# Running the shift matmuls of a block before the weight contraction of an older block on TensorE

## The reference

```python
value = (xf @ vp_w.T + vp_b).reshape(n, L, G, cg)
om_in = conv_general_dilated(x, dw_w, (1, 1), 'SAME', feature_group_count=c, ...) + dw_b
om = om_in... @ om_w.T + om_b            # per pixel, 8 groups, 9 taps: offsets y and x, mask
py = row + base_y + off_y;  px = column + base_x + off_x
y0 = floor(py);  x0 = floor(px);  ty = py - y0;  tx = px - x0
sampled = bilinear(value at y0, y0+1, x0, x0+1)   # zero outside the image
out = einsum('nhwgk,nhwgkc->nhwgc', mask, sampled)
out = out.reshape(n, L, c) @ op_w.T
```

## Time and profile before

| | |
|---|---|
| median of 3 runs | 2999.73 us (2999.16 to 3000.77) |
| profiled execution | 2998.01 us, span 2996.1 us |
| TensorE busy | 2713.6 us, 91% of the span |
| VectorE busy | 2195.8 us, 73% |
| ScalarE busy | 2107.3 us, 70% |
| GpSimd busy | 1924.4 us, 64% |
| first `windows` to last | 785 to 2962 us of the span |

### The profile page before, as it was taken

How to read it: one execution, slowest core, us unless ns; L and a number is a source line. 1 busy time by engine, 2 the same in 40 slices (tenths; PEclk the granted TensorE clock), 3 DMA queues, 4 the chain that set the end, 5 groups by cost and what they waited for, 6 DMA issues and landing times. The chain is left out here.

```text
span 2996.1 us, 99369 instructions
## 1 busy us (share of the span) xinstructions
PE 2713.6 (91%) x40456; PEld 2166.3 (72%) x40456; DVE 2195.8 (73%) x3108; ACT 2107.3 (70%) x4273; POOL 1924.4 (64%) x1451
## 2 busy tenths in 40 slices
PE   5888859996599999999999999999999999999998
PEld 3555536774388787877878787777778787778786
DVE  4454533334688897989898888989897988889763
ACT  2334326662778787887878787887878787878782
POOL 2000000001788888888988888888888888888892
PEclk9999979998799999999999999999999999999999
DMA  4344459995477777777778786777777787777675
GB/s 109 97 117 108 129 124 264 266 266 158 133 192 205 189 210 194 202 198 193 203 194 215 192 209 184 214 191 200 204 191 199 192 215 189 208 189 210 172 183 153
DMA packets 343609, 558.99 MB, mean 187 GB/s; under 512 B 159184, under 2 KB 245712, under 8 KB 342992
## 3 DMA queue, kind: packets, MB, share of 16 engines
q1 hardware_dynamic: 284112, 461.96, 61.2%
q10 hardware_dynamic: 59136, 91.76, 8.6%
HBM read 351.36 MB, written 202.19 MB: 185 GB/s over the span
## 5 line engine op out<-in xcount | busy, mean ns | idle before, releaser
L1277 PE MATMUL acc_p<-abuf,vbd 128*32 128x170 f32 (+9 forms) x20480 | 1033.4, 370 | 10.7 <-issue 9.6
L1277 PEld LDWEIGHTS acc_p<-abuf,vbd 128*32 128x32 f32 (+1 forms) x20480 | 819.4, 144 | 216.4 <-issue 30.0
L1110 ACT ACTIVATE dwt<-xp,wts 128x224 f32<-128x224 f32 x2016 | 803.1, 488 | 41.0 <-ACT wst L1134 32.3
L981 DVE TENSOR_TENSOR pr<-mh_p,ht 128x864 f32<-128x864 f32 x672 | 669.2, 1052 | 23.2
L243 PE MATMUL cv<-cin,wb 128*64 128x392 bf16 x6912 | 603.1, 338 | 26.0 <-ACT cin L222 26.0
L1254 PE MATMUL win_p<-pr,smat 128*128 128x160 f32 x4032 | 612.0, 306 | 12.6 <-POOL pr L1067 10.9
L1254 PEld LDWEIGHTS win_p<-pr,smat 128*128 128x128 f32 x4032 | 557.6, 191 | 38.5 <-issue 13.3
L243 PEld LDWEIGHTS cv<-cin,wb 128*64 128x64 bf16 x6912 | 409.7, 112 | 213.4 <-ACT cin L222 26.2
L1050 POOL TENSOR_TENSOR dwt<-dwt 128x896 f32<-128x896 f32 x224 | 518.8, 2316 | 4.7 <-ACT dwt L1110 4.7
L1064 POOL TENSOR_TENSOR pr<-pr 128x576 f32<-128x576 f32 x224 | 317.0, 1415 | 211.5 <-DVE pr L981 211.5
L971 DVE TENSOR_TENSOR mh_p<-oms,ht 128x864 f32<-128x864 f32 x224 | 395.3, 1765 | 7.1 <-ACT ht L1125 7.1
(11 more groups left out here) (132 smaller groups left out, 2581.2 us busy)
## 6 DMA issues: line engine op xcount, KB each, us to landing
abuf<-weight_scratch SPq DMA_DIRECT2D x784, 240.0 KB, 4.1
weight_scratch<-wst ACTq DMA_DIRECT2D x112, 800.0 KB, 5.1
xt<-x SPq DMA_DIRECT2D x128, 392.0 KB, 7.6
rows_scratch<-vsb SPq DMA_DIRECT2D x224, 128.0 KB, 3.1
vbd<-rows_scratch SPq DMA_DIRECT2D x896, 32.0 KB, 4.5
x_scratch<-xt SPq DMA_DIRECT2D x64, 392.0 KB, 6.7
y<-x SPq DMA_DIRECT2D x64, 392.0 KB, 5.3
x3h<-x_scratch SPq DMA_DIRECT2D x64, 392.0 KB, 5.7
```

Of the source, the lines that this page charges most:

```text
L981: dve.tensor_tensor(pr[:, j % 2, slots, :, :, :].rearrange("p k e x z -> p e k (x z)"), mh[:, a, :, :].rearrange("p (k x) z -> p k (x z)", ...
L1110: ins = act.activation(dwt[:, j % 2, k, :].rearrange("p (r w) -> p r w", w=W), image[:, r:r + BR, k % 3:k % 3 + W], ACT.Identity, scale=dw ...
L1277: mm = pe.matmul(acc_p[32 * (2 * s + b):32 * (2 * s + b) + 32, 0:2 * TN].rearrange("p (k w) -> p k w", w=W)[:, k0:k1 + 1, x0:x1], vbd[0:K, ...
```

## The change

In `step` of TensorE in `l1_pass` the call of `windows` moves ahead of that of `apply`:

```diff
                 def step(i, j, first, last):
+                    windows(i, j)
                     n = near(i, j, -5 if j % 2 else -4, first, last)
                     if n:
                         apply(*n, j % 2)
-                    windows(i, j)
                     offsets_and_misc(phase(i, j), i + 1 if j == GROUPS_AT and not last else None,
                                      near(i, j, 2, first, last), near(i, j, -LAG, first, last), near(i, j, 3, first, last))
```

## The result

| | median, us | runs, us | span of the profiled execution, us |
|---|---|---|---|
| before | 2999.44 | 4, 2996.04 to 3000.77 | 2996.1 |
| changed | 3039.76 | 4, 3035.53 to 3043.59 | 3035.8 |

The ratio is 1.0136 with a 95% interval of 1.0118 to 1.0153: some 41 us slower.

The account below looks back on a forecast made before the run. TensorE was taken as the bound, idling mostly before offsets_and_misc behind GpSimd's depthwise sum. Merge 27, load 21 and clock -2 sum to +46 us: 3044 for the profiled execution, 3046 as median, range 3013 to 3072.

Parts of the forecast that it names:

- clock, spells after: TensorE, step 9 after the change: spells at 1.2 GHz in 7 to 15 pairs, 0.95 us each; 10 us.
- clock, spells before: TensorE, step 9 before the change: seven spells at 1.2 GHz, 1.7 us lost each, credited to the change as -12 us.
- First step, the merge: Steps 9 and 10: windows, now first, waits for GpSimd's late merge; 1.79 us in each of 15 pairs, 27 us.
- Step 8 adds none: Step 8: no loss from the merge, since offsets_and_misc waits there for VectorE's L962, which comes at its old time.
- That step 4 costs nothing: Step 4 ends 1.32 us later, but mask_hats in step 5 still ends behind GpSimd's L1050; 0 us added.
- Second step, the load: SyncE, step 6: the next images' last quarter is issued some 3.5 us later, so VectorE waits in step 7; 21 us.
- if the transfers land as much faster: Lower bound of the load term: transfers issued later land correspondingly faster, so the load costs 0 instead of 21 us.
- Third step, the clock: TensorE around step 9: spells at 1.2 GHz before and after the change nearly cancel; -2 us, between -12 and +2.
- Rival 1: Step 7: the load lands in time anyway, leaving +25 us, 3025; chance 0.22.
- Rival 2: ScalarE's weight copies in odd steps become the wait, their cover being only 0.55 us; 3080 to 3100 us, chance 0.08.
- Rival 3: TensorE's waits only move from offsets_and_misc to windows, nothing to be seen: within 6 us of 3000; chance 0.07.
- Rival 4: VectorE's mask_hats falls between GpSimd's operations, 97 us less VectorE work in the backlog, so faster: 2949; chance 0.08.

Follow-up runs that it names:

- e6b: Changed kernel with step 6's image load issued ahead of its weight read and ten filling matmuls ahead of windows in step 9: 3011.61 us, ratio 1.0046.
- e1: Changed kernel with SyncE issuing step 6's load of the next images ahead of its weight read: 3022.17 us, ratio 1.0092.
- e2: Changed kernel with ten filling matmuls on TensorE ahead of windows in step 9: 3020.69 us, ratio 1.0088.
- e10: Kernel before with eight filling matmuls of 160 columns ahead of offsets_and_misc in step 9: 2998.60 us, ratio 1.0010.
- e4: Kernel before with the new order (windows ahead of apply) in step 9 of each pair alone: 3032.46 us, ratio 1.0127.
- e5b: Changed kernel with the old order (apply, then windows) in step 4 of each pair alone: 3035.12 us, ratio 1.0124.
- e3: Changed kernel with the old order (apply, then windows) in step 9 of each pair alone: 3023.22 us, ratio 1.0090.
- e9: Changed kernel with four filling matmuls on TensorE at the head of step 9: 3026.52 us, ratio 1.0100.

## Why the prediction held, point by point

The forecast was +46 us, 3046, and +41 was measured. The merge and the late load were right as mechanisms, and both were put too high; the clock was put at nothing on balance and costs some 10 us. So the near agreement of the sum is partly luck, since the errors cancel. The third column is from ratios, each term uncertain by some 7 us, the fourth from the lengths of pairs in the traces, times fifteen:

| term | predicted, us | ratios, us | traces, us | traces: from |
|---|---|---|---|---|
| merge | 27 | 14 (e6b) | 15 | e6b 137.90, before without spell 136.90 |
| load of step 6 | 21 | 13 (e1; e6b against e2) | 9 | e2 138.52, e6b 137.90 |
| clock, spells after | 10 | 14 (e2; e6b against e1) | 17 | changed 139.63, e2 138.52 |
| clock, spells before | -12 | none seen (e10) | -7 | seven of 0.96 each |
| sum | 46 | 41 | 34 | |

The 14 of the ratios in the first row is against a kernel with seven spells; free of them it would be some 7 more. The remaining 5 to 6 us of the 39.7 by which the span grew lie in the first and the last pair and outside the steps.

**First step, the merge.** Its size in steps 9 and 10 was right. Without spells and late load these two take 23.38 us (e6b), and before, in the pairs without a spell, 21.75: 1.63 a pair for the 1.79 predicted. The wait of step 9 was to be 3.5 to 4 us and is 3.58 in nearly all pairs of the changed kernel. What failed is the sentence "Step 8 adds none: M there waits for L962, which comes at its old time". L962 comes earlier: the waits of M for it fall from 25.8 us in 15 places to 10.2 in 8, step 8 is 10.93 us in e6b for 11.77, and steps 0 to 8 together are 87.11 for 87.63, so 0.52 a pair come back. Steps 0 to 8 are shorter because the merges of steps 2 to 8, but for step 6, follow each other about 0.1 us sooner each (9.86 for 9.95 in step 2, 9.82 for 9.98 in step 8); in e4, where these steps have the old order, they do not. GpSimd's L1050 takes 2.42 us for 2.50 in four of these steps and 2.09 for 2.13 to 2.18 in others. That the new phase of TensorE relieves GpSimd there fits this, but what they share was not tried: it stays open. So a pair costs 137.90 - 137.31 = 0.59 in e6b, 8 us for fourteen (1.00 against the pairs of before without a spell), and the first and last pair, which the prediction did not treat apart, 2.3 and 2.7; the remaining 2 us of the 15.5 by which e6b's span is longer lie outside the steps counted.

**That step 4 costs nothing** held, by the very rows that it named (e5b). The Trainium skill, page SBUF — State Buffer, section Who interferes with whom, has the exclusive lock behind it; 2.57 us against 1.18 with the same end agrees.

**Second step, the load.** The delay of the issue was to be some 3.5 us and was about 3.6. The bound "if the transfers land as much faster" was the part that mattered: from issue to landing the last load takes 6.78 us on average in place of 7.41, 0.6 faster. 21 less 0.6 in each of some 14 pairs is 12.6; VectorE waited 14.4, 0.96 a pair on average where 1.4 were forecast. What failed besides is "it passes on to the merge of step 9 in full": where the load is moved the merge of step 9 comes 0.6 us earlier (e1 against the changed kernel, e6b against e2), 9 us for fifteen pairs. The 13 us of the ratios can't be told from that.

**Third step, the clock.** This failed, and in an instructive place. Three things were wrong. The number: between 7 and 15 spells were taken, and it was 15. The price after: 1.7 less 0.75 hidden, 0.95, is for a spell of 3.4 us, and such a one costs 0.67; but ten of the fifteen lasted 6.8 us and cost 1.65 each. The credit: "1.7 us lost each, 12 in all" for the spells before. A low clock had been seen, and its lost matmul time was taken for lost time; by the trace such a spell made steps 9 and 10 longer by 1.03 and the pair by 0.96, 7 us in all. So the clock costs some 20 by steps 9 and 10 (17 by whole pairs) less 7, and not -2. The reading behind it was loose too: "the other 8 had waits of about as much" holds for four of them (2.52 to 2.61 us before M); the other four waited 0.95 to 1.97 there and had the rest of their idle time earlier in the step. And of the seven spells five follow a wait of 2.5 to 2.6 us before M; in the first and the twelfth pair TensorE stood idle inside A instead, for 2.42 and 1.71 us. The Trainium skill, page TensorE: Matmul & The Clock Gate, section Why this matters for your kernels, had all 15 by its rule on idle gaps; the trace agrees on the number.

**The rivals.** Rival 1, load in time, fell with the wait before L922. Rival 2, ScalarE, fell with 0.7 us of waits for L1134. Rival 3 fell on step 9. Rival 4 had a grain in it: `mask_hats` became shorter, 163 ns on the mean of 224, 36 us of VectorE work, but that is where its start was late already, so it gained nothing, in place of the 97 us that it needed.

## What to carry to other kernels

Where an engine has two pieces of work of which one needs a late input, the one that doesn't should stand first: it is the cover. What a spell of low clock cost here depended on the wait that followed: a short one cost about 1 us in the kernel before, where no wait followed, 0.67 where a wait of 0.75 us followed, and nothing where one of 1.77 us did (e3). So look at what stands behind a spell and not at its length alone. To price spells that only some rounds of a loop have, compare the rounds with and without one in the same trace; it told 1 us here where whole runs could not.

## What the runs showed of the hardware

- The same idle stretch before the same matmuls gives or doesn't give a spell from pair to pair: with 2.5 to 2.6 us before M (kernel before) 5 of 9 pairs, with 3.5 to 3.6 before W (changed) 15 of 15, with 1.48 and 0.79 us about four matmuls (e9) 5 of 15.
- Behind the wait of 3.58 us W takes 4.80 us on average for 2.7; filling that wait with ten matmuls made the kernel 14 us faster by the ratios and 19 by the spans, with 150 matmuls more (300 on its page: each of these float32 matmuls has two records).
- The spells of one kernel differ in length from pair to pair and from execution to execution: 3.4 or 6.8 us, ten long ones in the changed kernel, three in e1.
- Filling the wait of the kernel before with matmuls of 28 columns left seven spells in that step and two one step earlier, with as many of 160 columns none behind that wait, but three one step earlier.
- GpSimd's adds and merges became about 0.1 us a step shorter or closer when TensorE's W moved to the head of the step. No run here says by what.
